# Clearing the banks of the edge sums with a zero product of 128 rows in place of one row

## What is computed

```python
x = layernorm(x + gcn(x, edge_weight, ...))                 # two graph convolutions and a dense layer
x = layernorm(x + gat(x, src, dst, ...))                    # attention over the edges that enter a node
x = layernorm(x + typed(x, node_type, src, dst, edge_type, ...))   # the same with typed keys and values
x = layernorm(x + edges(x, src, dst, ...))                  # a gated product per edge
# in each: rows of the source node are gathered, worked on per edge, and summed over the edges of a node
msg = norm[:, None] * h[src]
agg = segment_sum(msg, dst, num_segments=N)
```

## Time and profile before

| | us |
|---|---|
| median of 3 runs | 8030.02 (8029.71 to 8035.61) |
| the profiled execution | 8034.67 |
| its span, first to last instruction | 8032.9 |
| PE busy in the span | 5711.9 (71%) |
| POOL busy | 4948.6 (62%) |
| DVE busy | 4513.4 (56%) |
| ACT busy | 3446.2 (43%) |
| mean granted clock of TensorE | 0.725 of full speed |

### The profile page before, as it was taken

How to read it: one execution, slowest core, us unless ns; L and a number is a source line. 1 busy time by engine, 2 the same in 40 slices (tenths; PEclk the granted TensorE clock), 3 DMA queues, 4 the chain that set the end, 5 groups by cost and what they waited for, 6 DMA issues and landing times. The chain is left out here.

```text
span 8032.9 us, 116503 instructions
## 1 busy us (share of the span) xinstructions
PE 5711.9 (71%) x27385; PEld 4167.4 (52%) x27386; DVE 4513.4 (56%) x11773; ACT 3446.2 (43%) x7679; POOL 4948.6 (62%) x4989
## 2 busy tenths in 40 slices
PE   6777775777775777764788887875666666677774
PEld 4565554444443444443667775434555543455553
DVE  7666664555555555555344444445666656556666
ACT  0222222444443444421556554444666632555552
POOL 0677775777776777744777771017777700677774
PEclk6555566888887888876555555996777768888886
DMA  1222221222232221122666663447777731666665
GB/s 36 60 51 51 51 51 48 51 51 52 51 49 57 52 51 51 51 33 78 167 165 171 169 167 70 147 146 212 228 231 229 227 71 57 208 201 200 201 202 134
DMA packets 809344, 920.12 MB, mean 115 GB/s; under 512 B 116834, under 2 KB 646762, under 8 KB 809002
## 3 DMA queue, kind: packets, MB, share of 16 engines
q0 software_dynamic: 198144, 441.54, 21.9%
q1 hardware_dynamic: 394794, 368.51, 15.3%
q10 hardware_dynamic: 216320, 109.07, 4.6%
HBM read 724.85 MB, written 193.87 MB: 114 GB/s over the span
## 5 line engine op out<-in xcount | busy, mean ns | idle before, releaser
L732 POOL DMA_INDIRECT arena<-t,stage_idx x3328 | 3257.5, 979 | 1257.1 <-issue 1003.2
L778 PE MATMUL ps<-arena 128*128 128x128 f32 (+2 forms) x8320 | 1994.7, 405 | 733.6 <-DMA arena<-t,stage_idx 621.6
L778 PEld LDWEIGHTS ps<-arena 128*128 128x128 f32 x8320 | 1616.9, 267 | 1177.2 <-issue 1122.2
L787 DVE TENSOR_TENSOR arena<-arena,ps 128x512 f32 (+2 forms) x1040 | 836.6, 804 | 1307.1 <-PE ps L778 1267.4
L688 POOL DMA_INDIRECT d_rec<-arena x784 | 781.1, 996 | 442.8 <-issue 251.5
L2365 POOL DMA_INDIRECT arena<-t,stage_idx x832 | 832.9, 1001 | 297.3 <-issue 222.4
L775 PE MATMUL ps<-int_tmp 1*128 1x256 bf16 (+2 forms) x2080 | 554.4, 355 | 483.4 <-DVE arena L787 217.4
L1613 PE MATMUL ps<-arena 128*128 x3328 | 651.9, 352 | 334.5 <-ACT arena L1515 317.7
L1613 PEld LDWEIGHTS ps<-arena 128*128 128x128 f32 x3328 | 640.4, 295 | 351.3 <-issue 351.1
L1163 PE MATMUL ps<-arena 128*128 128x416 f16 x3328 | 748.1, 378 | 0.0
L841 POOL TENSOR_TENSOR small<-small,neg_half 128x7 f32<-128x7 f32 x35 | 58.5, 1672 | 1000.8 <-DVEq L826 1000.8
(11 more groups left out here) (379 smaller groups left out, 8381.1 us busy)
## 6 DMA issues: line engine op xcount, KB each, us to landing
spill<-arena ACTq DMA_DIRECT2D x208, 512.0 KB
arena<-spill SPq DMA_DIRECT2D x208, 512.0 KB
arena<-t,stage_idx POOLq DMA_INDIRECT x4160, 3.3
arena<-d_loT SPq DMA_DIRECT2D x208, 256.0 KB
arena<-s_loT SPq DMA_DIRECT2D x104, 512.0 KB, 4.6
arena<-key_d SPq DMA_DIRECT2D x98, 512.0 KB
t<-arena SPq DMA_DIRECT2D x98, 512.0 KB, 2.9
d_rec<-arena POOLq DMA_INDIRECT x784
```

Of the source, the lines that this page charges most:

```text
L732: pool.indirect_dma_start(out=rows[r][:, i, :], out_offset=None, in_=table, in_offset=bass.IndirectOffsetOnAxis(ap=stage_idx[:, 8 * r + i: ...
L778: return nc.tensor.matmul(self.banks[i // 4][:, bass.ds(self.slot[i], self.width)], weights, rows, start=False, stop=False, skip_group_che ...
L787: nc.vector.tensor_tensor(at, at, got, ALU.add).then_inc(self.added, 1)
```

## The change

The zero operand and the zero weights of the clearing matmuls are taken from all 128 rows of the tile of zeros, in place of its first row. The number of instructions, their order on every engine, the waits and the columns are the same.

```diff
@@ -762,7 +762,7 @@
                 self.banks = [ps[:, (bank_of + 2 * z) * 512:(bank_of + 2 * z) * 512 + 4 * SLOT] for z in range(2)]
-                self.blank = bcast_mid(zeros16[0:1, 0:width], 2)
+                self.blank = bcast_mid(zeros16[:, 0:width], 2)
@@ -772,7 +772,7 @@
                     half = self.banks[z][:, 2 * SLOT * y:2 * SLOT * (y + 1)].rearrange("p (r f) -> p r f", f=SLOT)
-                    nc.tensor.matmul(half[:, :, 0:self.width], zeros16[0:1, 0:P], self.blank, start=True, stop=False, skip_group_check=True)
+                    nc.tensor.matmul(half[:, :, 0:self.width], zeros16[:, 0:P], self.blank, start=True, stop=False, skip_group_check=True)
```

## The result

The changed kernel takes 7935.87 us (median of 4 runs, 7928.32 to 7938.99) against 8029.86 us for the kernel before: a ratio of 0.9883, with a 95% interval of 0.9866 to 0.9900, or 94 us less. The forecast was 7952.5 us, 77.5 us less.

A forecast was written before the change was run, and what follows sets the result against it. POOL's gathers were taken to bound four of five edge passes and PE to bound gat. Savings of 60 us in gat, 17 in two pass ends and 0.5 elsewhere, 77.5 in all, gave 7952.5 us, range 7924 to 7990.

The forecast's parts named there:

- The bound: Four of the five edge passes go at POOL's pace; only gat goes at PE's, with nearly every weigh on the path.
- The cost of a pair: Clearing pair in gat: 2.67 us from pair to pair at the lower clock; full rows save 0.47, between 0.22 and 0.58.
- The way in: From four products' weight loads to the clearing pair's, lower clock: 2.11 us becomes 1.75, a saving of 0.36.
- The way out: From the clearing pair's loads to the next products' loads, lower clock: 0.56 us becomes about 0.34.
- Gat's sum: Gat up to its last look-up: PE's side 81 us, POOL's side 60; the smaller counts, so 60 us less.
- POOL's side: What POOL allows in gat: 47 us of standing still plus 13.5 of shrinking trail at the end, 60 us.
- The windows of 84 to 85 us: Gat's windows of eight halves, 89.3 us before, expected with carries 84 to 85 us apart after the change.
- The ends of the passes: After the last look-up, 12 weighs in gat and the same in typed attention: 8.4 us each, 17 for both.
- Elsewhere: Typed attention up to its last look-up and last layer 0, hidden by POOL; convolutions 0.5 us for both.
- Nothing changes: Rival: gaps around the pair come from accumulation start or address registers, so no gain; 8030 or 8039 us, chance 0.08.
- The clock rises in gat: Rival: PE's clock goes up, POOL caps the pass, two ends gain 14 us each; 7924 us, chance 0.05.
- Slower by the clock: Rival: PE stands still longer in POOL-bound passes, clock falls, mainly in the last layer; up to 8182 us, chance 0.05.

The follow-up runs named there:

- the doubled kernel: The changed kernel with each full-row clearing matmul issued twice, 4160 in all: 7965.41 us, 0.9906 of the kernel before.

## Why the prediction was right, and where it was off

In the prediction's own terms, each pass from its first gather, against the two traces:

| stretch | forecast, us less | measured, us less |
|---|---|---|
| gat, first gather to last look-up | 60 | 74.3 |
| gat, last look-up to last product | 8.4 | 10.7 |
| typed, first gather to last look-up | 0 | -5.4 (longer) |
| typed, last look-up to last product | 8.4 | 19.8 |
| the rest | 0.5 | 7.0 |

**The bound.** It held: POOL covers four passes, and PE was on gat's path. That gat has nearly all of the gain is shown by the kernels with 128 rows in one part only.

**The cost of a pair.** That the change of the products' shape costs the gap is shown by 64 against 65 rows. The size was 0.40 us, for the 0.47 taken. The way in came out nearly as the step without a gap had said: 1.82 us where it was 2.11, with 0.07 left of the 0.36. The way out was mis-sized: I had expected the next product's load to run beside the second clearing matmul, 0.34 us after the pair's load. It comes after 0.45, when both clearing matmuls have streamed; only the 0.11 beyond them went away.

**Gat's sum.** I took POOL's side as the smaller one, at 47 us of standing still, and said that it can't give more. It had more to give. From gat's first gather to its last POOL stood still for 67.4 us before and 14.5 after, 53 less. I had counted one wait behind 4811.5 us; there are two, and the second, 7.6 us, stands in the row of "issue":

```profile
POOL arena L732 <- issue: 15.5, 27, 7.6
POOL arena L732 <- DVE stage_idx L718: 5.5, 1, 5.5
```

The gathers got shorter too, 986 ns for 994, which is 6.7 us over 832, and I had held them fixed. The last look-up (4803.4) comes 6.7 us behind the last gather (4796.7), where 7.9 were expected from the earlier trace rows; that is 14.7 us less than before. 52.9 + 6.7 + 14.7 are the 74.3.

The windows of 84 to 85 us were a misreading. The nine windows before hold 587 gathers, but nine windows' work is 576: POOL was still running ahead of PE there. 576 x (0.993 + 0.304) = 747 us, or 83.0 a window, and the shorter gathers make it 82.5. The windows are 82.4.

By PE's side 16 x 0.40 = 6.4 us a window would give 58 us over the nine, of the 62 that went. So the missing gaps alone would, by this estimate, nearly do; but in the doubled kernel the clock gave PE at least some 7 us a window, so the clock alone might have done much of it as well. Which of the two brought how much of the 74 us stays open.

**The ends of the passes.** This term was too small, above all in typed attention: 10.7 and 19.8 us for 8.4 each. (The 12.8 and 12.7 of the table further up run from the last carry and not from the last look-up.) One reason is in my counting. Behind the last look-up stand 13 weighs and not 12, 26 pairs, and the pass goes on to 4980.9 us; the last row is not its last product. Yet 26 pairs at 0.40 us are 10.4 us even if all were on the path, so at least 9 us in typed attention came from something else. The clock is the likely cause, and not isolated: it was 0.52 in both ends before. After, in the stretches that hold the two ends, it is 0.69 and 0.74:

```profile
4784.00:4890.00 106.00, 58.88 (x320) 52.95 (x321) 49.62 (x93) 62.04 (x165) 10.37 (x11) 0.69 0.49 91
6366.00:6465.00 99.00, 52.80 (x305) 46.79 (x305) 52.89 (x91) 56.87 (x153) 0.00 (x0) 0.74 0.38 88
```

And two rows of PE near gat's end after, with its wait for DVE's add, which itself stands behind the reload of a spilled message:

```profile
4888.72 0.61 PE L775 MATMUL ps<-int_tmp 128*128 128x272 bf16 x2 [3.98 <-DVE arena L787]
4889.13 2.02 PE L778 MATMUL ps<-arena 128*128 128x136 f32 x8
```

**Elsewhere.** Half a microsecond was forecast for the convolutions and none for the last layer; it is 3.2 up to gat's first gather, and 4.0 in the last layer's gathers. The typed pass, whose gathers I had expected as long as before, takes 6.6 us more from its first gather to its last (983 ns each for 975). That is 1063.2 us before and 1069.8 after, and it is 1068.1 in the kernel that has 128 rows in gat only, so most of it does not seem to come from the full rows of this pass. Why it is longer stays open.

**The rivals.** *Nothing changes* fell with the first rows of the trace. *The clock rises in gat* had a chance of 0.05, and came true beside the forecast rather than in place of it: I had made them exclusive, and that was the error, since the edit puts 127 more rows to work whatever the gaps do. What it was worth isn't isolated. Its price (28 us) was for the two ends, which gained 31 together, with at most 21 of it from the gaps. A faster PE runs into something else there: the reload of a spilled message, behind which PE waits for line 787 for 3.4 to 4.0 us near gat's end, where before it was 2.0 at most. *Slower by the clock* did not come: in the stretches read, the clock rose in gat, typed attention and the last layer, and stayed at 0.83 in the convolution.

So the bound and the gap were right by their reasons, and part of the agreement in the number was luck: a pair that saved less than forecast was made up for by a POOL with more time to give than I had read, and by the clock.

## What to carry to other kernels

Look also for the pass in which that engine is on the path: of 1040 pairs those in gat and at the end of typed attention brought nearly all of the gain, since the gathers hid the rest. And when the work of one engine is to be held against a stretch, count its pieces first: nine windows had 587 gathers in them where 576 were due.

## What the runs showed of the chip

TensorE's granted clock was higher where its clearing products used more rows, though all of them were zeros: in gat 0.50 with one row, 0.67 with 128 and 0.72 with 128 rows and each clearing matmul twice, on chips where the kernel takes 8030 and 8038 us; on the slow chips 0.50 with one row and each twice, 0.55 with 64 rows, and 0.59 to 0.61 with 128 rows and a change of shape. And three chips gave 8038, 9684 and 9814 us for the same kernel; in the kernels traced on the two slow ones there are idle stretches of 1 to 2.5 us between products that no engine or transfer of the profile accounts for.
